# Softmax weights scaled before the value products instead of after them, and the MLP's first products taken as three single-pass products

## The reference, cut to what matters

```
h = shift_token(x);  q, k, v = split(h @ wqkv)          # 8 heads of 64
q, k = rotary(l2norm(q) * qs, l2norm(k) * ks)
for each window of 64 queries:                            # keys: its own window and the one before
    p = softmax(8 * q @ k.T, masked);  o = p @ v
x = x + o @ wo
h = layernorm(shift_token(x)) * g + b
a, gate = split(h @ w1 + b1)                              # 341 columns each
x = x + (a * gelu(gate)) @ w2 + b2
```

## Time and profile before

| what | value |
|---|---|
| median of three runs | 1000.57 us (1000.53 to 1000.77) |
| the profiled execution | 1000.6 us, its span 998.5 us |
| PE busy | 939.0 us |
| DVE busy, ACT busy | 732.4 us, 728.0 us |
| POOL busy | 386.4 us |
| granted TensorE clock, mean | 0.996 |

### The profile page before, as it was taken

One profiled execution on the slowest core, in us unless ns is written; L12 is line 12 of the kernel. 1 busy time (PEld: TensorE's weight loads), 2 busy tenths in 40 slices (PEclk: granted clock), 3 DMA queues, 4 the chain that ended last, 5 costly groups with the idle time before them and its releaser, 6 DMA issues.

```text
span 998.5 us, 22947 instructions
## 1 busy us (share of the span) xinstructions
PE 939.0 (94%) x8744; PEld 575.5 (58%) x8744; DVE 732.4 (73%) x1218; ACT 728.0 (73%) x1563; POOL 386.4 (39%) x272
## 2 busy tenths in 40 slices
PE   8999999999789999999999999999999999999985
PEld 4333333333566676666766566666666666766752
DVE  6887878886487777777777677777677777777741
ACT  3577777778688786877867677777778868788662
POOL 2110113123366536455443534434355454544411
PEclk9999999999999999999999999999999999999999
DMA  2210100000211101011000101000011011110100
GB/s 82 66 40 10 26 2 2 3 1 2 59 29 28 24 18 33 18 28 23 18 23 17 23 18 23 17 13 22 18 23 29 18 26 25 23 39 17 34 22 11
DMA packets 23303, 23.72 MB, mean 24 GB/s; under 512 B 8626, under 2 KB 15068, under 8 KB 23196
## 3 DMA queue, kind: packets, MB, share of 16 engines
q1 hardware_dynamic: 23196, 22.27, 9.3%
HBM read 6.16 MB, written 1.05 MB: 7 GB/s over the span
## 4 chain that ended last, share of the span: by engine, by line
PE 54%; DVE 10%; ACT 5%; issue 3%; POOL 1%; DVEq 0%; POOLq 0%; ACTq 0%
PE psum L1381 8%; PE psum L1350 6%; PE psum L1292 5%; PE psum L1389 4%; PE psum L1313 4%; PE psum L1302 3%; PE psum L1264 3%; PE psum L1253 3%; DVE BS L1619 3%; PE psum L1374 3%; PE psum L1255 3%; PE psum L1254 3%; DVE A L1615 3%; PE psum L1368 2%; PE psum L1277 2%
## 5 line engine op out<-in xcount | busy, mean ns | idle before, releaser
L1182 POOL TENSOR_TENSOR A<-A,BS 128x1024 f32<-128x1024 f32 x62 | 146.2, 2359 | 207.1 <-DVE BS L1619 206.9
L878 DVE TENSOR_REDUCE a_M<-psum 128x2 f32<-128x1024 f32 x128 | 155.3, 1220 | 34.0 <-PE psum L651 33.2
L1187 POOL TENSOR_TENSOR A<-A,RN 128x1024 f32<-128x1024 f32 x62 | 117.9, 1902 | 89.5 <-ACT RN L1511 86.0
L1496 ACT ACTIVATE f_PW<-psum,f_NM 128x128 f32<-128x128 f32 x512 | 138.5, 381 | 18.7 <-DVE f_NM L1651 18.7
L774 ACT ACTIVATE a_PT<-psum 128x1024 f32<-128x1024 f32 x128 | 128.8, 1020 | 23.2 <-PE psum L661 23.0
L1615 DVE TENSOR_TENSOR A<-psum,cos 128x512 f32<-128x512 f32 x124 | 84.8, 684 | 35.1 <-ACT SQ L1462 35.1
L1651 DVE TENSOR_REDUCE f_NM<-psum 128x4 f32<-128x512 f32 x128 | 82.1, 683 | 38.5 <-PE psum L1292 38.5
L1462 ACT ACTIVATE SQ<-psum 128x512 f32<-128x512 f32 x124 | 72.1, 624 | 49.4 <-PE psum L1255 46.4
L1381 PE MATMUL psum<-f_mid,w 128*128 128x512 f32 (+1 forms) x192 | 87.0, 603 | 2.7 <-DVE f_mid L1681 2.7
L1313 PEld LDWEIGHTS psum<-f_VS,f_PT 128*64 128x64 f32 x1024 | 64.5, 137 | 38.8 <-issue 38.3
L1619 DVE TENSOR_TENSOR BS<-psum,sin 128x512 f32<-128x512 f32 x124 | 84.2, 679 | 0.0
(11 more groups left out here) (212 smaller groups left out, 1946.1 us busy)
## 6 DMA issues: line engine op xcount, KB each, us to landing
f_VS<-V SPq DMA_DIRECT2D x112, 130.0 KB, 2.3
raw<-L_ffn_wqkv_dram SPq DMA_DIRECT2D x2, 768.0 KB, 4.8
a_XT<-L_attn_a_x_dram SPq DMA_DIRECT2D x4, 256.0 KB, 2.9
out_dram<-f_OUT SPq DMA_DIRECT2D x4, 256.0 KB, 2.3
w<-L_ffn_w_dram SPq DMA_DIRECT2D x2, 341.0 KB
tables<-const_dram SPq DMA_DIRECT2D x1, 512.0 KB, 3.7
wo<-L_ffn_wo_dram SPq DMA_DIRECT2D x8, 64.0 KB
const<-const_dram SPq DMA_DIRECT2D x1, 264.0 KB, 3.1
```

The source lines that it names most:

```text
L878: nc.vector.tensor_reduce(M[:, quads % 2, t, 2 * j:2 * j + 2], psum[:, pair("scores", i), :], AX_X, ALU.max).then_inc(s("maxed"), 1)
L1182: nc.gpsimd.tensor_tensor(A[:, k % 2, :, :], A[:, k % 2, :, :], BS[:, k % 2, :, :], ALU.add)\
L1187: nc.gpsimd.tensor_tensor(x, x, RN[:, k % 2, :, None].to_broadcast([P, 2 * HW, DW]), ALU.mult)\
L1496: last = nc.scalar.activation(PW[:, u % 4, c, :], psum[:, bank("scores", u), P * c:P * c + P], ACT.Exp, bias=NM[:, u % 4, c:c + 1])
```

## The change

The softmax weights are now divided by their sum before the value products. New stage weigh: DVE sums the rows of PW for both halves of a tile (one reduction of 128x1024 to 128x8) and takes a reciprocal, POOL multiplies PW by it (128x1024). So the products of sums can take the values as weights and PT as the moving operand: their result is already feature by token, the layout that wo needs. The ones column, the division (RD, ON) and turn_o with its transposes are gone; ACT's copy to OT now reads the result of sums. The number of matrix instructions of sums stays, with 64 columns instead of 65. turn_p and its copies move one step later (lag 2 to 3) and open the step; sums moves to lag 3 behind project.

In the MLP, center_mlp becomes two single-pass products and each of the six products of w1 becomes three. For that POOL now writes mid_h and mid_l (two copies as before, two one-column copies for the memset, and two new subtractions of 64x512 and 64x511), DVE's norm has three instructions for two, and w1 is split once into high and low parts (ACT at step 4, POOL at step 5). The weights w1 lie in the memory of gates until then.

```diff
     "PE": [("latent", 8, of_sequence), ("turn_p", 3, of_tile), ("turn_p_2", 3, of_tile),
+           ("project", 0, of_tile), ("features_b", 10, of_sequence), ("sums", 3, of_tile), ("turn", 1, of_tile),
...
+                    elif stage == "weigh":
+                        k = i
+                        pool.wait_ge(s("den_recip"), k + 1)
+                        x = PW[:, 2 * (k % 2):2 * (k % 2) + 2, :, :].rearrange("p u c x -> p (u c) x")
+                        nc.gpsimd.tensor_tensor(x, x, RD[:, k % 2, :, None].to_broadcast([P, 2 * PAIRS, P]), ALU.mult)\
+                            .then_inc(s("weighed"), 1)
...
-                        nc.gpsimd.tensor_copy(mid[0:64, :], Y[0:64, n, :]).then_inc(s("shifted_mid"), 1)
-                        pool.wait_ge(s("shifted_mid"), 2 * i + 1)
-                        nc.gpsimd.tensor_copy(mid[64:P, 1:T], Y[64:P, n, 0:T - 1]).then_inc(s("shifted_mid"), 1)
...
+                        for half, (rows, to, of) in enumerate(SHIFTED):
+                            nc.gpsimd.tensor_copy(mid_h[rows, to], Y[rows, n, of]).then_inc(s("mid_high"), 1)
+                            pool.wait_ge(s("mid_high"), 3 * i + half + 1)
...
+                        for half, (rows, to, of) in enumerate(SHIFTED):
+                            pool.wait_ge(s("mid_low"), 3 * i + half + 1)
+                            nc.gpsimd.tensor_tensor(mid_l[rows, to], Y[rows, n, of], mid_h[rows, to].bitcast(F32),
+                                                    ALU.subtract).then_inc(s("mid_low"), 1)
...
                 def turn_p(u):
-                    pe.wait_ge(s("exped"), u + 1)
+                    pe.wait_ge(s("weighed"), u // 2 + 1)
...
                 def sums(k):
                     pe.wait_ge(s(f"moved{k % 4}"), moved(k))
...
+                    dst = take("sums", k).rearrange("p (c x) -> p c x", c=PAIRS)
+                    pe.wait_ge(s("p_copied"), k + 1)
+                    pe.wait_ge(s("p_copied_2"), k + 1)
+                    for c in range(PAIRS):
+                        for w, values in ((0, VS), (1, V)):
+                            for j in range(2):
                                 last = nc.tensor.matmul(
-                                    dst[WIN * w:WIN * w + WIN, c, :], PT[:, u % 4, c, WIN * w:WIN * w + WIN],
-                                    values[:, k % 4, 2 * c + j, :], start=True, stop=True)
...
+                                    dst[DW * j:DW * j + DW, c, WIN * w:WIN * w + WIN],
+                                    values[:, k % 4, 2 * c + j, :],
+                                    PT[:, (2 * k + j) % 4, c, WIN * w:WIN * w + WIN], start=True, stop=True)
...
+                                nc.tensor.matmul(dst, w1_h[:, layer, of], mid_h[:, :], start=True, stop=False)
+                                nc.tensor.matmul(dst, w1_h[:, layer, of], mid_l[:, :], start=False, stop=False)
+                                nc.tensor.matmul(dst, w1_l[:, layer, of], mid_h[:, :], start=False, stop=True)\
+                                  .then_inc(s(kind), 1)
...
+                    elif stage == "weigh":
+                        k = i
+                        dve.wait_ge(s("exped"), 2 * k + 2)
...
+                        nc.vector.tensor_reduce(RD[:, k % 2, :], x, AX_X, ALU.add).then_inc(s("den"), 1)
+                        dve.wait_ge(s("den"), k + 1)
+                        nc.vector.reciprocal(RD[:, k % 2, :], RD[:, k % 2, :]).then_inc(s("den_recip"), 1)
```

More of the change, by code:

```diff
@@ L994 @@
            ("var_mlp", 4, of_group), ("var_a", 3, of_first), ("var_b", 7, of_sequence),
-           ("var_y", 10, of_sequence), ("w2", 6, of_group), ("wo", 3, of_group), ("sums", 2, of_tile), ("store", 6, of_end)],
-    "ACT": [("latent", 8, of_sequence),
-            ("squares", 0, of_tile), ("features_b", 10, of_sequence), ("turn", 1, of_tile), ("features_a", 1, of_first), ("values", 0, of_tile), ("turn_o", 3, of_tile),
+           ("var_y", 10, of_sequence), ("w2", 6, of_group), ("wo", 3, of_group), ("store", 6, of_end)],
@@ L998 @@
+    "ACT": [("turn_p", 3, of_tile), ("latent", 8, of_sequence),
+            ("squares", 0, of_tile), ("features_b", 10, of_sequence), ("values", 0, of_tile), ("sums", 3, of_tile),
+            ("turn", 1, of_tile), ("features_a", 1, of_first),
             ("center_mlp", 4, of_group), ("center_a", 3, of_first), ("center_b", 7, of_sequence),
-            ("center_y", 10, of_sequence), ("split", SEQS, of_tile), ("w1", 5, of_group), ("turn_p", 2, of_tile), ("keys_b", 8, of_sequence),
+            ("center_y", 10, of_sequence), ("split", SEQS, of_tile), ("w1", 5, of_group), ("keys_b", 8, of_sequence),
@@ L1004 @@
+    "DVE": [("lead", 0, of_lead), ("turn_p_2", 3, of_tile), ("weigh", 2, of_tile), ("latent", 8, of_sequence),
+            ("rope", 0, of_tile), ("project_a", 2, of_first), ("context", 9, of_sequence), ("project_b", 10, of_sequence),
+            ("w1", 5, of_group), ("keys_b", 8, of_sequence), ("soften", 1, of_tile),
             ("tokens_b", 9, of_sequence), ("var_mlp", 4, of_group), ("var_a", 3, of_first),
-            ("var_b", 7, of_sequence), ("var_y", 10, of_sequence), ("wo", 3, of_group),
@@ L1044, in stream @@
     norms, number = number_norms()
+    done_mlp = [sum(use == "mlp" for use, _ in norms[:x]) for x in range(len(norms))]
     order = []
@@ L1051, in stream @@
             order += [("turned_q", i), ("turned_k", i)]
-        elif stage in ("scores", "sums", "keys_b", "tokens_b"):
+        elif stage in ("scores", "keys_b", "tokens_b"):
             order += [(stage, 2 * i), (stage, 2 * i + 1)]
@@ L1063, in stream @@
             order += [("var", number[stage[4:], i])]
-        elif stage in ("turn_o", "wo", "w2", "context", "features_b", "project_b", "store", "features_a", "project_a"):
+        elif stage in ("sums", "wo", "w2", "context", "features_b", "project_b", "store", "features_a", "project_a"):
             order += [(stage, i)]
@@ L1367, in _ @@
                             x = X[:, j, :]
-                        nc.tensor.matmul(take("center", number[use, j]), cst("center"), x, start=True, stop=True)\
-                          .then_inc(s("center"), 1)
+                        dst = take("center", number[use, j])
+                        if use == "mlp":
+                            nc.tensor.matmul(dst, centre[:, :], mid_h[:, :], start=True, stop=False)
+                            last = nc.tensor.matmul(dst, centre[:, :], mid_l[:, :], start=False, stop=True)
+                        else:
+                            last = nc.tensor.matmul(dst, cst("center"), x, start=True, stop=True)
+                        last.then_inc(s("center"), 1)
                     elif stage[:4] == "var_":
```

142 lines of the change are left out of this document (65 added, 77 removed).

## The result

The changed kernel takes 1050.74 us (median of 4) against 1000.67 for the kernel before on the same chip: **4.8% slower**, ratio 1.0476 with a 95% interval of 1.0428 to 1.0524. One of its runs, at 1259.09 us, had a mean granted clock of 0.649 and is left out of the ratio. The forecast was 989 us, in a range of 958 to 1012. The profiled execution took 1050.74 us, its span is 1048.9.

What follows compares the result with a forecast made beforehand. PE was taken as the bound, busy 939.0 of 998.5 us. Eleven groups at -9, four with attention b at -5, and ends at +3.6 were summed as -11 from 1000.6: 989 us, range 958 to 1012 for 8 in 10.

Steps and rivals of the forecast that it cites:

- A: One of a group's four steps, each from one project to the next: 10.5 us forecast, 10.90 before.
- B: The step of a group with the MLP's centring and variance product: 8.05 us forecast, 8.68 before.
- D: The step of a group that opens behind w1 and the scores: 10.35 us forecast, 10.25 before.
- Step D's sums: PE's sums there would come 0.7 us late, waiting for ACT's copy of turn_p behind the exponentials.
- the loop of DVE and ACT: Rival: exponentials, weigh, rope and norm become the bound, 1022 us; chance 0.22 with its milder forms.
- step C's wait: Sums in the step with w1 wait for DVE's copy of turn_p behind the norm: 1.4 us, from 1.1 to 1.9.
- POOL will now mostly be: Caution on DVE's norm: its second instruction took 0.98 us instead of 0.49 where POOL was at work beside it.
- the drain: End of the pipeline: weigh, POOL's subtractions and the norm stand bare, w1 gives 1 us back; +3.6 us.
- the groups with attention b: Four groups of 54.29 us: -1.2 us each, -5 together, with center_y waiting about 1 us more for DVE.
- POOL and DVE in each other's way: Rival: POOL's new product slows DVE or is slowed by a half, 1 us per tile; 1021 us, chance 0.05.
- The fill: Start of the pipeline: splitting w1 costs ACT 1.5 and POOL 3.3 us, half hidden; turn_o gone returns 2; net 0.
- Centring in two: center_mlp as two single-pass products: 0.45 us less PE work at best, 0.1 us wait for mid_h and mid_l.

Runs made afterwards that it cites:

- e5: Changed kernel with useless bf16 products on PE ahead of the wait of sums, in two steps of each group: 1040.86 us.
- e2: Changed kernel with DVE's three norm instructions reading the centred product in PSUM, the first writing back there: 1047.48 us.
- e6: Changed kernel with sums behind turn on PE, and its copy behind turn's on ACT: 1020.71 us.
- e11: e10 with the centring again one fp32 product of a mid that POOL writes with two copies; w1 still in three products: 981.70 us.
- e1: Changed kernel with POOL making the low parts of the weights behind weigh and scale instead of ahead: 1044.63 us.
- e9: e8 with POOL's low parts of the weights behind weigh and scale, and attention b's output multiplied ahead of sums and added ahead of rope: 987.97 us.
- e10: e6 with POOL's low parts of the weights behind weigh and scale, and e9's order in the steps of attention b: 1009.78 us.
- e8: Changed kernel with the MLP as before the change (softmax part alone) and sums behind turn: 1012.15 us.

## Why the prediction was wrong

**What it had right.** The steps without a surprise came near the forecast: A 10.75 (10.5), B 8.17 (8.05), D 10.46 (10.35). w1's block takes 4.35 us from 465.14 to 469.49 in the clean group (4.3). Step D's sums wait 0.71 for ACT's copy (0.7). The scores wait 0.40 for KT (0.65). weigh is hidden once the pipeline runs: turn_p waits for it 6 times, twice 2.61 us in the fill and four times 0.20 later, so the loop of DVE and ACT, my heaviest rival with 0.22, is not what made it slow.

**The step that failed first: step C's wait and what it does to the clock.** I took 1.4 us of a range of 1.1 to 1.9; PE stands 1.84 to 1.90 in most quiet groups and 2.46 to 2.48 in three. The term that was mis-sized is DVE's norm: its second instruction, put at 0.49, measured 1.34, and its third, put at 0.75, measured 2.27 in the groups with the longest waits. The caution about it, "POOL will now mostly be" at work, had moved the sum by 0.3 us and not by 0.85. At full clock a quiet group is then 42.2 and not 40.95, a gain turned into a loss of 0.4: step C 0.76 over the forecast, the other three steps 0.48 together. What I did not have at all is that a wait of this length ahead of work can halve PE's clock for some 3 us of that work: 1.6 us more in most quiet groups, and more in the drain and in the groups with attention b. e5 shows it by filling the wait; and in e2 and e6, where PE's wait in step C is shorter (1.63 and 0.67 us), the clock never falls in a quiet group. All of PE's 45 us of saved work were priced at full clock. PE was busy for 71 us at half clock and before for 6; at full clock the same work takes half as long, so busy time would have fallen by some 41 us and not by 9 (an estimate). In e11, nearly free of half clock, it fell by 32 us (939.0 to 907.2), with the centring's work left in.

By the prediction's own terms: the nine groups without attention b behind the first two, put at -7, came out at +19; the first two and the start, put at next to nothing, at +14; the groups with attention b, put at -5, at +6; the drain, put at +3.6, at +11.4. No single term explains the 50 us. (The terms as written add up to -10 and not -11, and the drain's to +4.0; neither matters here.)

**The rival that was nearest** is "POOL and DVE in each other's way", which had 0.05 and 1021 us. I dismissed it because none of DVE's instructions per tile but the reduction is new. The kind that it needs comes once a group: an instruction with its one source in SBUF, which was there already and now has POOL at work beside it, and the new third one, with two sources in SBUF, which my argument passed over. Its price of a hold in every tile did not come: what was held is the norm, once a group. The rule of the Trainium skill that I cited (GPSIMD Engine Reference, Specifications) agrees with the trace where the rows can show it: the instruction with two inputs in SBUF took 2.27 beside POOL's product and 0.75 without. For the second instruction the rows show 0.49 alone, 1.34 beside POOL's product and 0.75 from PSUM beside the same product; in which mode it ran they do not say.

**The fill, put at nothing or half hidden,** cost 13.8 us. e1 shows 5 to 6 of it to be weigh queued behind the low parts of the weights on POOL; I had counted split_w1's duration and not what is queued behind an instruction that waits. e9, with the orders and without the MLP part, has 33.55 and 41.69 there, less than before; so the rest goes with the order of the sums and with the MLP part, but how it divides was not taken apart.

**The drain, put at +3.6,** was +11.4. The waits are long enough there to halve the clock. The two longest are 5.17 us ahead of the last centring (at 1027.00, where POOL's chain for mid had ended 0.10 before) and 4.51 ahead of the sums, behind a copy of DVE that stands behind the norm; of the latter PE, and the norm's third instruction:

```profile
995.32 0.49 PE L1329 MATMUL psum<-f_PT,f_VS 128*64 128x64 f32 x4 [4.51 <-DVE f_PT L1664]
```

```profile
992.30 2.27 DVE L1703 SCALAR_TENSOR_TENSOR f_mid_l<-f_ln_squared,vecs,f_mid_h 128x512 fp32r<-128x512 f32 x1
```

It took 2.27 us for 0.75; POOL's product ran from 992.12 to 994.02, and the instruction ended 0.55 behind it. e11's drain is 59.1, so +3.5; but e11 also has another order and lacks the subtractions, for which the +3.6 had counted 2.5, so that it equals the forecast is luck.

**The groups with attention b, put at -1.2 each,** came out at +1.1 to +2.6. I named the wait of center_y behind weigh and rope and put it at 1 us; it is 2.4, 9.5 us in the four groups together, and behind one of them the clock fell too (step D 16.82 for 15.24). At the end of step B of these groups PE waits 2.44 us to take the bank that the norm reads, a wait that I had not looked for, and behind it the clock fell in all four groups (at 553.7, 608.3, 662.9 and 721.0).

**Centring in two,** counted at -0.45 on PE and +0.1 of wait, "It just fits", did fit in the changed kernel as far as PE's wait for it goes: 0.15 us in the clean group. What I left out is what the chain holds up on POOL: I checked it against the one product that needs it, and not against weigh and scale, which POOL does next, and through scale the norm on DVE. With the sums behind turn PE comes to the centring earlier and stands 0.85 us for it. e10 against e11 prices the centring at 28 us in that order; in the order of the changed kernel it was not tested by itself.

What stays open: how the part of the 28 us that lies outside the quiet groups divides between POOL's delay itself and the clock behind the waits it makes; how the 50 us divide between waits and clock, beyond the rough 19 for the clock; and why e8's runs spread by 13 us.

## What to carry to other kernels

A saving on the engine that bounds is worth what its order keeps covered: write down, for each instruction taken away, which handoff stood behind it as cover, and give the place to other work (here sums behind turn, 30 us). Check a chain that moves to a helper engine against what is queued behind it there and not only against its consumer, and cut a saving that is small on PE and long on the helper (here 0.45 us against 28). Here a wait of about 2 us on PE cost up to nearly twice itself, by the clock; price such waits in both ways, and read the granted clock before busy times are compared.

## What the hardware showed that I had not expected

DVE's tensor_scalar with its source and its output in SBUF (128x512) took 0.49 us alone and 1.34 in the median beside POOL's products, ending 0.28 us behind these; from PSUM it took 0.75 in all sixteen, and a product of POOL ran beside it in fourteen of them. The scalar_tensor_tensor with two sources in SBUF took 0.75 in the median, and 2.27 to 2.28 in four of sixteen, where POOL's product had started just under 0.2 us before it. In these runs a tile read by the first was cheaper in PSUM if POOL was at work, and dearer if not.

PE's clock went to half behind single waits of 1.8 to 2.5 us and not behind each of them: of the waits of 1.84 and 1.90 us in two neighbouring groups the first was followed by half clock and the second was not. What decides this the runs do not show. A useless product put into the wait kept the clock up and made the kernel 1% shorter.
